# A graph block on one Trainium2 core: transpositions that write columns four apart, straight copies, and late work at other units

## The chip, the cores and the metric

The kernel runs on one core of a Trainium2 chip. TensorE (PE in the rows) multiplies matrices into PSUM, VectorE (DVE), ScalarE (ACT) and GpSimd (POOL) do elementwise work, SyncE (SP) issues transfers. Each engine runs its own list of instructions in order and waits on semaphores. The metric is the device time in microseconds (us), the median of several runs.

## The reference

```python
h = relu(layernorm(x))                       # x: 8192 x 128, fp32
deg = clip(adj.sum(axis=1), 1.0)             # adj: 8192 x 8192, zeros and ones
dis = deg ** -0.5
diffusion = (dis[:, None] * adj * dis[None, :]) @ h - h
norms = maximum(norm(h, axis=-1), 1e-8)
sim = h @ h.T / (norms[:, None] * norms[None, :])
attn = softmax(beta * sim * adj, axis=1)     # 8192 x 8192, over whole rows
out = x + diffusion + sigmoid(alpha) * (attn @ h - h)
```

## The kernel before, in words

The rows of x are cut into 64 tiles of 128. The first phase walks over 512 **units**: a panel of 1024 output rows (8 panels) against one tile of 128 rows. For unit n TensorE computes the 128 x 1024 cosines into one of two halves ("slots") of `cos_ps` (`cosines`, L814: six products with 512 columns, since each operand is split in two fp16 parts). VectorE multiplies them by the adjacency (`masked`, L696), ScalarE takes the exponential twice (L420 as fp16, L424 as fp32), GpSimd makes the fp16 rest of it (`rest`, L323), and TensorE adds 24 small products of these with h to `top_ps` (`sums`, L859 to L863). TensorE does `sums` of a unit three units after its `cosines` (LAG = 3). A second phase (L889) multiplies by the adjacency.

The cosines need **unit rows**, the rows of h divided by their norms, transposed. Eight tiles are one block. For a block VectorE or ScalarE writes the unit rows, TensorE transposes the eight tiles into a free slot of `cos_ps` (`transposed`, L790), and VectorE copies the slot to `uT_hi` (L609, a cast to fp16) and the remainder to `uT_lo` (L610). This is `copy_uT`. The copies also put the columns in an order in which every fourth column belongs together: they write every fourth fp16 value.

Only blocks 0 and 1 are made before the units begin; half of x is normalised by then. The rest is **late work**, put between the units by a table of unit numbers in each engine's loop: on VectorE the statistics of x and h (`stats_of_x`, `stats_of_h`, `mean_var`), the square sums (`late_square_sums`), the inverse roots by three Newton steps (`late_norms`, `late_shift`), the unit rows of a block (`late_unit_rows`, L597 and L598) and its copies; on ScalarE the normalising activations (`relu`, L365), first guesses of roots (L355) and the fp16 part of h (`head_of_h`, L375); on GpSimd `tail_of_h`. Such work sits behind the unit's own instructions and ahead of the next unit's. In steady state VectorE also turns a quarter of an adjacency chunk every fourth unit (L633) and sums rows in two of four (L640).

`AHEAD = {10: 2, 13: 3, 49: 4, ...}` says at which unit a block is transposed: at unit n TensorE waits until unit n-2 is masked, transposes the block into the slot that is free, computes the cosines of n into the other one once unit n-1 is masked, and may compute those of n+1 only when VectorE has copied the block out. TensorE can't be two units ahead of VectorE there. The scratch columns of PSUM that the late steps use are `late_ps`.

Of the kernel before, what the change touches and what calls it, by code (L numbers as in the profile page):

```python
# [5 lines left out]
P = 128  # L6
# [6 lines left out]
def gnn_block_kernel(nc, x, adj, alpha, beta, out):  # L13
# [8 lines left out]
    ALU = mybir.AluOpType  # L22
# [17 lines left out]
    READY = 2  # L40
    LAG = 3
# [7 lines left out]
    AHEAD = {10: 2, 13: 3, 49: 4, 52: 5, 65: 6, 68: 7}  # L49
# [21 lines left out]
    with ctx:  # L71
# [114 lines left out]
        u_ready = sem("u_ready")  # L186
        uT_done = sem("uT_done")
# [37 lines left out]
        def _(sp):  # L225
# [27 lines left out]
            for m in range(BLOCKS):  # L253
# [3 lines left out]
                if m in (12, 15):  # L257
                    keep_h(2 if m == 12 else 3)
# [30 lines left out]
        def _(pool):  # L289
# [40 lines left out]
            tails = {6: 4, 8: 5, 10: 6, 12: 7, 46: 8, 48: 9, 50: 10, 52: 11, 60: 12, 62: 13, 64: 14, 66: 15}  # L330
# [13 lines left out]
        def _(act):  # L344
# [32 lines left out]
            def unit_rows(hb):  # L377
                act.wait_ge(rnorm_ready, hb // 2 + 1)
                for s in range(8):
                    last = nc.scalar.activation(unit[hb][:, s, :], x_st[:, 8 * hb + s, :], ACT.Copy,  # L380
                                                scale=rnorm[:, 8 * hb + s:8 * hb + s + 1])
                last.then_inc(u_ready, 1)
# [12 lines left out]

            def copy_acc(run):
                panel, _, behind = RUNS[run]
                act.wait_ge(attn_done, 16 * behind)
                if run in (0, 4):

                    groups = 1 if run == 0 else CH
                    for g in range(groups):
                        act.wait_ge(h_kept[g], 16 * Q)
                    act.wait_ge(hlo_ready, 4 * groups)
                    act.wait_ge(u_ready, 2 * groups)
# [7 lines left out]
            for n in range(UNITS):  # L413
# [59 lines left out]
        def _(dve):  # L473
# [81 lines left out]
            def late_root(value, root, tmp, to):  # L555
                near = late_ps[:, 0:value.shape[-1]]
                link(nc.vector.tensor_copy(near, root))
                for step in range(3):
                    link(nc.vector.scalar_tensor_tensor(out=tmp, in0=value, scalar=-0.5, in1=near, op0=ALU.mult, op1=ALU.mult))
                    link(nc.vector.tensor_tensor(tmp, tmp, near, ALU.mult))  # L560
                    last = nc.vector.scalar_tensor_tensor(out=near if step < 2 else to, in0=tmp, scalar=1.5, in1=near,
                                                          op0=ALU.add, op1=ALU.mult)
                    if step < 2:
                        link(last)
                return last

            def late_shift():
                of = slice(32, TILES)
                dve.wait_ge(std_ready, 3)
                link(late_root(va[:, of], vb[:, of], vc[:, of], rstd[:, of]))  # L570
                link(nc.vector.tensor_copy(late_ps[:, 0:32], rstd[:, of]))
                nc.vector.scalar_tensor_tensor(out=shift[:, of], in0=mv[:, of, 0], scalar=-1.0, in1=late_ps[:, 0:32],
                                               op0=ALU.mult, op1=ALU.mult).then_inc(ln_ready, 1)
                dve.wait_ge(ln_ready, 3)

            def late_square_sums(g):
                of = slice(16 * g, 16 * (g + 1))
                link(mean_var_of_h(g))
                both = late_ps[:, 0:32].rearrange("p (s k) -> p s k", k=2)
# [6 lines left out]
            def late_norms(g):  # L586
                of = slice(16 * g, 16 * (g + 1))
                dve.wait_ge(norm_root, g + 1)
                late_root(ssq[:, of], vb[:, of], vc[:, of], rnorm[:, of]).then_inc(rnorm_ready, 1)
                dve.wait_ge(rnorm_ready, g + 1)  # L590

            def late_unit_rows(hb):
                of = slice(8 * hb, 8 * (hb + 1))
                dve.wait_ge(rnorm_ready, hb // 2 + 1)
                if hb > READY:
                    dve.wait_ge(uT_done, hb)
                link(nc.vector.tensor_copy(late_ps[:, 0:8], rnorm[:, of]))  # L597
# [331 lines left out]
```

## Time and profile before

| | |
|---|---|
| median of 3 runs | 1914.03 us (1913.74 to 1915.01) |
| profiled execution | 1914.11 us, span 1912.0 us |
| PE busy | 1834.0 us, 96% |
| DVE, ACT, POOL busy | 1269.6, 1278.5, 1271.4 us, 66 to 67% each |
| granted TensorE clock, mean | 0.992 |

Durations are of one profiled execution. The time of a run is the span and 2.1 us around it. A row's time runs from start to end of an instruction, and the ends overlap the next start a little: an instruction with a row of 1.22 us lets the next one start after 1.14 us. The masks (L696) count the units: the first is unit 0, and the n-th after it unit n.

### The profile page before, as it was taken

To read this page: it belongs to the slowest core of one execution; us is meant where nothing else is said; L and a number is where in the kernel's file an instruction comes from. 1 tells how busy PE (TensorE), PEld (TensorE's weight loads), DVE (VectorE), ACT (ScalarE), POOL (GpSimd) and SP (SyncE) were. 2 spreads that over 40 slices of the span, in tenths; PEclk is the share of its full clock that TensorE was granted. 3 is DMA by queue.
4 is the path that set the end of the run, shared out by engine and by line. 5 is a ranking of instruction groups with operands and counts; after the bars stand their busy time and mean duration, and the time that the engine had idled before them with its cause. 6 is when DMAs were issued, how large, how long until landed. Compare 5 with 4: busy or idle time off the path is not lost.

```text
span 1912.0 us, 44763 instructions
## 1 busy us (share of the span) xinstructions
PE 1834.0 (96%) x19534; PEld 1448.1 (76%) x19534; DVE 1269.6 (66%) x1590; ACT 1278.5 (67%) x1210; POOL 1271.4 (66%) x793
## 2 busy tenths in 40 slices
PE   1899889999999999999999999999999999999999
PEld 1576567777777777777777777777777888888888
DVE  6988997879878778777877877787777210111111
ACT  4689868888889888988988898899887000000000
POOL 4688779998999999999999999999883000000000
PEclk9999989999999999999999999999999999999999
DMA  9977657876798876788887767888536745554520
GB/s 155 154 100 97 99 76 99 105 105 89 100 114 101 107 100 90 100 98 105 103 105 102 100 89 101 99 106 101 116 89 232 248 173 180 170 200 166 208 101 12
DMA packets 190409, 229.39 MB, mean 120 GB/s; under 512 B 7940, under 2 KB 163588, under 8 KB 186116
## 3 DMA queue, kind: packets, MB, share of 16 engines
q0 software_dynamic: 135168, 67.13, 44.9%
q1 hardware_dynamic: 29380, 145.77, 20.7%
q10 hardware_dynamic: 25664, 13.63, 2.6%
q8 instruction: 153, 2.51, 0.5%
q14 instruction: 44, 0.36, 0.1%
HBM read 352.32 MB, written 75.50 MB: 224 GB/s over the span
## 4 chain that ended last, share of the span: by engine, by line
PE 88%; DVE 6%; ACT 3%; issue 1%; DMA 0%; SPq 0%; DVEq 0%; ACTq 0%
PE cos_ps L814 32%; PE cos_ps L889 12%; PE top_ps L889 12%; PE top_ps L859 11%; PE top_ps L863 11%; PE top_ps L861 11%; DVE xe L696 1%; ACT xe L424 1%; ACT ustage L420 1%; DVE uT_lo L610 1%; DVE uT_hi L609 1%; ACT asb L365 1%; DVE top_ps L640 1%; DMA asb<-x_in 0%; DVE ptmp L598 0%
## 5 line engine op out<-in xcount | busy, mean ns | idle before, releaser
L323 POOL TENSOR_TENSOR ustage<-xe,ustage 128x1024 f16<-128x1024 f32 x512 | 1096.7, 2145 | 163.3 <-ACT xe L424 156.4
L696 DVE TENSOR_TENSOR xe<-cos_ps,arena 128x1024 f32<-128x1024 f32 x512 | 626.6, 1224 | 253.6 <-PE cos_ps L814 160.9
L420 ACT ACTIVATE ustage<-xe,ebias,ab 128x1024 f16<-128x1024 f32 x512 | 635.6, 1241 | 173.2 <-DVE xe L696 169.1
L859 PE MATMUL top_ps<-h,ustage 128*128 128x129 f16 x4096 | 722.6, 221 | 7.8 <-POOL ustage L323 5.5
L863 PE MATMUL top_ps<-h,ustage 128*128 128x129 f16 x4096 | 722.1, 221 | 0.0
L861 PE MATMUL top_ps<-hlo,ustage 128*128 128x128 f16 x4096 | 721.7, 220 | 0.0
L424 ACT ACTIVATE xe<-xe,ebias,ab 128x1024 f32<-128x1024 f32 x512 | 628.6, 1228 | 0.0
L859 PEld LDWEIGHTS top_ps<-h,ustage 128*128 128x128 f16 x4096 | 402.1, 98 | 72.1 <-POOL ustage L323 17.2
L861 PEld LDWEIGHTS top_ps<-hlo,ustage 128*128 128x128 f16 x4096 | 402.1, 98 | 56.2 <-issue 0.8
L863 PEld LDWEIGHTS top_ps<-h,ustage 128*128 128x128 f16 x4096 | 402.1, 98 | 0.0
L814 PE MATMUL cos_ps<-uT_hi 128*128 128x512 f16 x1024 | 307.0, 382 | 23.7 <-DVE uT_lo L610 21.7
L640 DVE TENSOR_REDUCE top_ps<-arena 128x8 f32<-128x1024 uint16 x256 | 311.8, 1218 | 0.0
L814 PE MATMUL cos_ps<-uT_hi,uT_lo 128*128 128x512 f16 x1024 | 307.0, 382 | 0.0
L814 PE MATMUL cos_ps<-uT_lo,uT_hi 128*128 128x512 f16 x1024 | 306.5, 381 | 0.0
L814 PEld LDWEIGHTS cos_ps<-uT_lo,uT_hi 128*128 128x128 f16 x1024 | 116.4, 114 | 106.6 <-issue 2.7
L814 PEld LDWEIGHTS cos_ps<-uT_hi,uT_lo 128*128 128x128 f16 x1024 | 116.6, 114 | 106.2 <-issue 2.2
L302 POOL DMA_DIRECT2D arena<-adj_in_dram x256 | 171.2, 670 | 7.4 <-DMA asb<-x_in 7.4
L633 DVE STREAM_TRANSPOSE arena<-arena 128x1024 uint32<-128x1024 uint32 x128 | 158.0, 1234 | 0.0
L770 DVE SCALAR_TENSOR_TENSOR ptmp<-top_ps,dis,ptmp 128x128 f32<-128x128 f32 x64 | 19.5, 346 | 189.4 <-PE top_ps L889 188.8
L770 DVE SCALAR_TENSOR_TENSOR ptmp<-cos_ps,dis,ptmp 128x128 f32<-128x128 f32 x64 | 19.5, 347 | 158.6 <-PE cos_ps L889 158.0
L814 PEld LDWEIGHTS cos_ps<-uT_hi 128*128 128x128 f16 x1024 | 87.3, 113 | 27.3 <-DVE uT_lo L610 23.0
L889 PE MATMUL cos_ps<-uT_hi,arena 128*128 128x256 f16 x896 | 100.1, 275 | 2.8 <-DVE uT_hi L751 2.8
(110 smaller groups left out, 1044.8 us busy)
## 6 DMA issues: line engine op xcount, KB each, us to landing
arena<-adj_in_dram POOLq DMA_DIRECT2D x256, 256.0 KB, 8.4
at_scratch<-arena SPq DMA_DIRECT2D x128, 512.0 KB, 4.2
arena<-at_scratch SPq DMA_DIRECT2D x26, 2048.0 KB, 7.9
xe<-at_scratch SPq DMA_DIRECT2D x6, 2048.0 KB, 7.8
h_scratch<-asb SPq DMA_DIRECT2D x16, 256.0 KB, 11.2
arena<-h_scratch SPq DMA_DIRECT2D x16, 256.0 KB, 6.5
ustage<-h_scratch ACTq DMA_DIRECT2D x8, 512.0 KB, 5.3
ptmp<-x_in ACTq DMA_DIRECT2D x8, 512.0 KB, 6.8
```

The source lines that it names most:

```text
L302: pool.dma_start(rows8[k % RS][C * q:C * (q + 1), of, :], adj_v[panel][:, of, 2048 * ch + 512 * q:2048 * ch + 512 * (q + 1)]).then_inc(row ...
L323: nc.gpsimd.tensor_tensor(elo[:, n % ES, :], ef[:, n % XS, :], ehi[:, n % ES, :], ALU.subtract).then_inc(elo_done, 1)
L420: nc.scalar.activation(ehi[:, n % ES, :], xm[:, n % XS, :], ACT.Exp, bias=ebias[:, 0:1], scale=ab[:, 1:2]).then_inc(ehi_done, 1)
L424: nc.scalar.activation(ef[:, n % XS, :], xm[:, n % XS, :], ACT.Exp, bias=ebias[:, 0:1], scale=ab[:, 1:2]).then_inc(ef_done, 1)
L633: nc.vector.transpose(at_words[:, w, :].rearrange("p (a r) -> p a r", r=32), rows_words[k % RS][:, :, 32 * w:32 * (w + 1)]).then_inc(at_re ...
L640: nc.vector.tensor_reduce(out=pairs_ps[:, of], in_=rows_pairs[k % RS][:, 8 * part:8 * (part + 1), :], axis=AX.X, op=ALU.add).then_inc(rows ...
L696: nc.vector.tensor_tensor(xm[:, n % XS, :], cos_ps[:, slot_of(n), :], at8[:, m % W, :, n % B], ALU.mult).then_inc(x_done, 1)
L814: last = nc.tensor.matmul(cos_ps[:, slot_of(n), q * HALF:(q + 1) * HALF].rearrange("p (w z) -> p w z", w=W), own(mine, s), columns(src, pa ...
L859: nc.tensor.matmul(top_ps[:, bank, col:col + P + 1], head, h1[:, s, 0:P + 1], start=(first and t % 3 == 0), stop=final, skip_group_check=True)
L861: nc.tensor.matmul(top_ps[:, bank, col:col + P], head, hlo[:, s, :], start=False, stop=final, skip_group_check=True)
L863: last = nc.tensor.matmul(top_ps[:, bank, col:col + P + 1], tail, h1[:, s, 0:P + 1], start=False, stop=final, skip_group_check=True)
L889: return nc.tensor.matmul(acc2[panel % 2][:, t, :], slot8[k % SL][:, j // B, t * P:(t + 1) * P, j % B], y[s // 32][:, s % 32, :], start=(s ...
```

## The change

`copy_uT` writes straight, and the transpositions write every fourth column of the PSUM slot instead. The two first blocks of unit rows are made by two engines: block 0 by VectorE in one instruction, block 1 by ScalarE in eight, where ScalarE made both. Their order against other work of the start changes. The late work has other unit numbers: `AHEAD` is {18: 2, 22: 3, 56: 4, 60: 5, 73: 6, 77: 7}, `relu` comes one tile a unit over 32 units instead of two over 16, statistics of h too, the Newton steps one a unit. TensorE gets 40 fp32 products of the identity with itself (128 columns) into slot 0 of `cos_ps` before the first transposition, once the first 16 tiles are normalised.

```diff
+    WARM = 40
-    AHEAD = {10: 2, 13: 3, 49: 4, 52: 5, 65: 6, 68: 7}
+    AHEAD = {18: 2, 22: 3, 56: 4, 60: 5, 73: 6, 77: 7}
...
@@ ScalarE
             var_root(0)
-            relu(0, 0, 8)
-            relu(0, 8, 16)
+            relu(0, 0, 16)
             var_root(1)
-            relu(1, 0, 8)
             ssq_root(0)
-            unit_rows(0)
-            unit_rows(1)
+            second_unit_rows()
             head_of_h(0)
             head_of_h(1)
-            relu(1, 8, 16)
+            relu(1, 0, 16)
...
-                elif n == 33:
+                elif n == 24:
                     var_root(2, 2)
-                if 35 <= n < 43:
-                    relu(2, 2 * (n - 35), 2 * (n - 34))
-                elif 48 <= n < 56:
-                    relu(3, 2 * (n - 48), 2 * (n - 47))
+                if 29 <= n < 45:
+                    relu(2, n - 29, n - 28)
+                elif 45 <= n < 61:
+                    relu(3, n - 45, n - 44)
@@ VectorE
+            def first_unit_rows():
+                dve.wait_ge(rnorm_ready, 1)
+                nc.vector.tensor_tensor(unit[0], x_st[:, 0:8, :], rnorm[:, 0:8].unsqueeze(2).to_broadcast([P, 8, P]),
+                                        ALU.mult).then_inc(u_ready, 1)
...
             def copy_uT(hb, slot):
                 dve.wait_ge(uT_done, hb + 1)
-
                 of = slice(PW * hb, PW * (hb + 1))
-                src = cos_ps[:, slot, :].rearrange("d (w b y) -> d w b y", w=2, b=B)
-                hi = uT_hi[:, of].rearrange("d (w y b) -> d w b y", w=2, b=B)
-                lo = uT_lo[:, of].rearrange("d (w y b) -> d w b y", w=2, b=B)
-                link(nc.vector.tensor_copy(hi, src))
-                nc.vector.tensor_tensor(lo, src, hi, ALU.subtract).then_inc(uT_copied, 1)
+                link(nc.vector.tensor_copy(uT_hi[:, of], cos_ps[:, slot, :]))
+                nc.vector.tensor_tensor(uT_lo[:, of], cos_ps[:, slot, :], uT_hi[:, of], ALU.subtract).then_inc(uT_copied, 1)
...
-            stats_of_h(0, 0, 8)
-            early_shift(1)
-            stats_of_h(0, 8, 16)
+            for four in range(4):
+                stats_of_h(0, 4 * four, 4 * (four + 1))
             early_square_sums(0)
             early_norms(0)
-            stats_of_h(1, 0, 8)
+            first_unit_rows()
+            early_shift(1)
             copy_uT(0, 0)
             copy_uT(1, 1)
...
-                if 1 <= n < 5:
-                    stats_of_h(1, 2 * n + 6, 2 * n + 8)
-                elif 16 <= n < 32:
-                    g, o = 2 + (n - 16) // 8, (n - 16) % 8
+                if 1 <= n < 9:
+                    stats_of_h(1, 2 * n - 2, 2 * n)
+                elif 31 <= n < 47:
+                    stats_of_h(2, n - 31, n - 30)
+                elif 48 <= n < 64:
+                    stats_of_h(3, n - 48, n - 47)
+                if 6 <= n < 22:
+                    g, o = 2 + (n - 6) // 8, (n - 6) % 8
...
+                elif n in (12, 13, 14):
+                    late_norms(1, n - 12)
+                elif n in (50, 51, 52):
+                    late_norms(2, n - 50)
+                elif n in (67, 68, 69):
+                    late_norms(3, n - 67)
...
-                elif n in (8, 11, 47, 50, 63, 66):
-                    late_unit_rows({8: 2, 11: 3, 47: 4, 50: 5, 63: 6, 66: 7}[n])
+                elif n in (15, 19, 53, 57, 70, 74):
+                    late_unit_rows({15: 2, 19: 3, 53: 4, 57: 5, 70: 6, 74: 7}[n])
@@ TensorE
                 for t in range(8):
-                    last = nc.tensor.transpose(cos_ps[:, slot, t * P:(t + 1) * P], unit[hb][:, t, :], ident32[:, :])
+
+                    dst = cos_ps[:, slot, HALF * (t // B):HALF * (t // B + 1)].rearrange("d (y b) -> d b y", b=B)[:, t % B]
+                    last = nc.tensor.transpose(dst, unit[hb][:, t, :], ident32[:, :])
                 last.then_inc(uT_done, 1)
...
+            pe.wait_ge(relu_done, 16)
+            for k in range(WARM):
+                nc.tensor.matmul(cos_ps[:, 0, 0:P], ident32[:, :], ident32[:, :], start=True, stop=True)
             transposed(0, 0)
             transposed(1, 1)
```

VectorE around the first late block (block 2), before the change, from the mask of unit 8 to that of unit 10:

```order
L696 TENSOR_TENSOR xe<-cos_ps,arena 128x1024
L640 TENSOR_REDUCE top_ps<-arena 128x8
L597 COPY top_ps<-rnorm 128x8
L598 TENSOR_TENSOR ptmp<-asb,top_ps 128x1024
L696 TENSOR_TENSOR xe<-cos_ps,arena 128x1024
L633 STREAM_TRANSPOSE arena<-arena 128x1024
L609 CAST uT_hi<-cos_ps 128x2x4x128
L610 TENSOR_TENSOR uT_lo<-cos_ps,uT_hi 128x2x4x128
```

and of the change, from the unit rows in unit 15 to the mask of unit 18 (L693 is the mask, L606 and L607 the copies, L508 statistics of x):

```order
L598 COPY top_ps<-rnorm 128x8
L599 TENSOR_TENSOR ptmp<-asb,top_ps 128x1024
L693 TENSOR_TENSOR xe<-cos_ps,arena 128x1024
L637 TENSOR_REDUCE top_ps<-arena 128x8
L508 BN_STATS ptmp<-asb 128x6 x2
L693 TENSOR_TENSOR xe<-cos_ps,arena 128x1024
L630 STREAM_TRANSPOSE arena<-arena 128x1024
L508 BN_STATS ptmp<-asb 128x6 x2
L606 CAST uT_hi<-cos_ps 128x1024
L607 TENSOR_TENSOR uT_lo<-cos_ps,uT_hi 128x1024
L693 TENSOR_TENSOR xe<-cos_ps,arena 128x1024
```

Between unit rows and copies stand two masks now, where one stood; the copies' shape is flat; statistics of x stand in between.

ScalarE while the second half of x is normalised, before (units 35 to 37: two exponentials, then two tiles):

```order
L420 ACTIVATE ustage<-xe,ebias,ab 128x1024
L424 ACTIVATE xe<-xe,ebias,ab 128x1024
L365 ACTIVATE asb<-asb,shift,rstd 128x128 x2
L420 ACTIVATE ustage<-xe,ebias,ab 128x1024
L424 ACTIVATE xe<-xe,ebias,ab 128x1024
L365 ACTIVATE asb<-asb,shift,rstd 128x128 x2
```

and of the change (units 45 and 46, where a `head_of_h`, L377, stands too):

```order
L418 ACTIVATE ustage<-xe,ebias,ab 128x1024
L422 ACTIVATE xe<-xe,ebias,ab 128x1024
L377 ACTIVATE h<-asb 128x8x128
L367 ACTIVATE asb<-asb,shift,rstd 128x128
L418 ACTIVATE ustage<-xe,ebias,ab 128x1024
L422 ACTIVATE xe<-xe,ebias,ab 128x1024
L367 ACTIVATE asb<-asb,shift,rstd 128x128
```

Every unit has one tile now, and the run of such units is twice as long.

## Rows read from the trace of the kernel before

**Rows 1.** Windows: us from:to, length, busy (x instructions) by engine, PEclk, DMA, GB/s
```profile
47.41:121.02 73.61, 65.14 (x641) 46.42 (x640) 66.86 (x100) 55.62 (x51) 51.40 (x29) 0.93 0.80 121
121.02:298.35 177.33, 157.81 (x1684) 115.44 (x1682) 161.11 (x273) 145.65 (x154) 145.40 (x93) 0.97 0.73 100
298.35:1434.00 1135.65, 1134.76 (x12843) 863.55 (x12841) 907.93 (x792) 1020.65 (x872) 1038.56 (x629) 1.00 0.74 101
```

**Rows 2.** Waits of TensorE: who waited for whom, us in total, times, longest
```profile
PE cos_ps L814 <- DVE uT_lo L610: 21.7, 7, 7.7
```

**Rows 3.** Timeline of the start: start us, us, engine, line, names, count, idle before
```profile
15.93 6.26 ACT L365 ACTIVATE asb<-asb,shift,rstd 128x128 f32<-128x128 f32 x16 [2.12 <-DVE shift L527]
...
24.48 1.64 DVE L533 BATCH_NORM_STATS2 ptmp<-asb 128x6 f32<-128x128 f32 x8
...
26.14 1.17 DVE L538 BATCH_NORM_AGGREGATE hv<-ptmp 128x2 f32<-128x6 f32 x16
...
30.20 4.78 ACT L380 ACTIVATE xe<-asb,rnorm 128x128 f32<-128x128 f32 x16 [1.92 <-DVE rnorm L486]
...
32.79 1.94 PE L790 MATMUL cos_ps<-ident,xe 128*128 128x128 f32 x8 [28.44 <-ACT xe L380]
...
44.55 1.04 PE L814 MATMUL cos_ps<-uT_hi 128*128 128x512 f16 x2 [7.67 <-DVE uT_lo L610]
...
47.41 1.23 DVE L696 TENSOR_TENSOR xe<-cos_ps,arena 128x1024 f32<-128x1024 f32 x1 [1.86 <-PE cos_ps L814]
```

**Rows 4.** Timeline of VectorE, units 8 to 10
```profile
72.66 1.22 DVE L598 TENSOR_TENSOR ptmp<-asb,top_ps 128x1024 f32<-128x1024 f32 x1
73.92 1.22 DVE L696 TENSOR_TENSOR xe<-cos_ps,arena 128x1024 f32<-128x1024 f32 x1
75.06 1.23 DVE L633 STREAM_TRANSPOSE arena<-arena 128x1024 uint32<-128x1024 uint32 x1
76.22 2.44 DVE L609 CAST uT_hi<-cos_ps 128x1024 f16<-128x1024 f32 x1
...
80.93 1.24 DVE L696 TENSOR_TENSOR xe<-cos_ps,arena 128x1024 f32<-128x1024 f32 x1
```

**Rows 5.** Products with 128 fp32 rows of `degs` (four in the code), L831: ns min/median/max
```profile
L831 PE MATMUL top_ps<-degs,ptmp x8: 219/275/275, 1439.3 to 1440.1; 128*128 128x64 f32 x8
```

**Rows 6.** Window with TensorE's clock at half, around the first cosines
```profile
40.05:50.30 10.25, 5.75 (x14) 2.06 (x15) 8.16 (x6) 1.56 (x2) 0.31 (x1) 0.50 1.15 234
```

**Rows 7.** Timeline of TensorE: cosines of units 17 and 18; block 4 transposed
```profile
103.34 0.59 PE L814 MATMUL cos_ps<-uT_hi 128*128 128x512 f16 x2
103.78 0.59 PE L814 MATMUL cos_ps<-uT_lo,uT_hi 128*128 128x512 f16 x2
...
105.99 0.59 PE L814 MATMUL cos_ps<-uT_hi 128*128 128x512 f16 x2
...
194.90 1.07 PE L790 MATMUL cos_ps<-ident,ptmp 128*128 128x128 f32 x8 [2.33 <-DVE ptmp L598]
```

**Rows 8.** Timeline of VectorE: statistics of x; masks of units 23 and 78
```profile
104.52 0.48 DVE L510 BATCH_NORM_STATS2 ptmp<-asb 128x6 f32<-128x128 f32 x2
...
121.02 1.22 DVE L696 TENSOR_TENSOR xe<-cos_ps,arena 128x1024 f32<-128x1024 f32 x1 [0.76 <-PE cos_ps L814]
...
298.35 1.22 DVE L696 TENSOR_TENSOR xe<-cos_ps,arena 128x1024 f32<-128x1024 f32 x1 [0.27 <-DVE arena L633]
```

**Rows 9.** Timeline of ScalarE, units 35 and 36
```profile
158.82 0.86 ACT L365 ACTIVATE asb<-asb,shift,rstd 128x128 f32<-128x128 f32 x2
159.59 1.23 ACT L420 ACTIVATE ustage<-xe,ebias,ab 128x1024 f16<-128x1024 f32 x1
...
161.86 0.86 ACT L365 ACTIVATE asb<-asb,shift,rstd 128x128 f32<-128x128 f32 x2
```

**Rows 10.** The page's costliest groups: GpSimd's fp16 rest
```profile
L323 POOL TENSOR_TENSOR ustage<-xe,ustage 128x1024 f16<-128x1024 f32 x512 | 1096.7, 2145 | 163.3 <-ACT xe L424 156.4
```

**Rows 11.** One line: a cast of 512 columns to fp16, out of SBUF, L750
```profile
L750 DVE CAST uT_hi<-ptmp x8: 426/427/428, 1457.5 to 1465.7; 128x512 f16<-128x512 f32 x8
```

More of the change, by code:

```diff
@@ L186, in gnn_block_kernel @@
         u_ready = sem("u_ready")
+        u1_ready = sem("u1_ready")
         uT_done = sem("uT_done")
@@ L256, in _ @@
                 sp.dma_start(at_dram[m // W, :, 1024 * w:1024 * (w + 1)], at_words[:, w, :]).then_inc(at_stored[w], 16)
-                if m in (12, 15):
-                    keep_h(2 if m == 12 else 3)
+                if m in (13, 16):
+                    keep_h(2 if m == 13 else 3)
                 if m // W in (CHUNKS - 3, CHUNKS - 2) and w == W - 1:
@@ L327, in first_unit @@
                 return 16 * (k - RS) + (18 if k < 13 else 13)
-            tails = {6: 4, 8: 5, 10: 6, 12: 7, 46: 8, 48: 9, 50: 10, 52: 11, 60: 12, 62: 13, 64: 14, 66: 15}
+            tails = {7: 4, 9: 5, 11: 6, 13: 7, 48: 8, 50: 9, 52: 10, 54: 11, 64: 12, 66: 13, 68: 14, 70: 15}
             for n in range(UNITS):
@@ L375, in head_of_h, with second_unit_rows @@
                 nc.scalar.activation(h1[:, 8 * hb:8 * (hb + 1), 0:P], x_st[:, 8 * hb:8 * (hb + 1), :], ACT.Copy).then_inc(hhi_ready, 1)
[L377 to L382, printed above, removed]
+            def second_unit_rows():
+                act.wait_ge(rnorm_ready, 1)
+                for s in range(8, 16):
+                    last = nc.scalar.activation(unit[1][:, s - 8, :], x_st[:, s, :], ACT.Copy, scale=rnorm[:, s:s + 1])
+                last.then_inc(u1_ready, 1)
             var_root(0)
-            relu(0, 0, 8)
-            relu(0, 8, 16)
+            relu(0, 0, 16)
             var_root(1)
-            relu(1, 0, 8)
             ssq_root(0)
-            unit_rows(0)
-            unit_rows(1)
+            second_unit_rows()
             head_of_h(0)
             head_of_h(1)
-            relu(1, 8, 16)
+            relu(1, 0, 16)
             def copy_acc(run):
@@ L552, in early_norms, with late_step @@
                 refine_root(ssq[:, of], vb[:, of], vc[:, of], rnorm[:, of]).then_inc(rnorm_ready, 1)
-            def late_root(value, root, tmp, to):
+            def late_step(value, root, tmp, to, step):
                 near = late_ps[:, 0:value.shape[-1]]
[L557 to L565, printed above, removed]
@@ L567, in late_shift @@
-            def late_shift():
-                of = slice(32, TILES)
[L569 to L574, printed above, removed]
+                if step == 0:
+                    link(nc.vector.tensor_copy(near, root))
@@ new lines, in late_step, with late_scale @@
+                link(nc.vector.scalar_tensor_tensor(out=tmp, in0=value, scalar=-0.5, in1=near, op0=ALU.mult, op1=ALU.mult))
+                link(nc.vector.tensor_tensor(tmp, tmp, near, ALU.mult))
+                link(nc.vector.scalar_tensor_tensor(out=near if step < 2 else to, in0=tmp, scalar=1.5, in1=near,
+                                                    op0=ALU.add, op1=ALU.mult))
+            def late_scale(step):
+                of = slice(32, TILES)
+                if step == 0:
+                    dve.wait_ge(std_ready, 3)
+                if step < 3:
+                    late_step(va[:, of], vb[:, of], vc[:, of], rstd[:, of], step)
+                else:
+                    link(nc.vector.tensor_copy(late_ps[:, 0:32], rstd[:, of]))
+                    nc.vector.scalar_tensor_tensor(out=shift[:, of], in0=mv[:, of, 0], scalar=-1.0, in1=late_ps[:, 0:32],
+                                                   op0=ALU.mult, op1=ALU.mult).then_inc(ln_ready, 1)
+                    dve.wait_ge(ln_ready, 3)
@@ L576, in late_square_sums @@
             def late_square_sums(g):
                 of = slice(16 * g, 16 * (g + 1))
-                link(mean_var_of_h(g))
-                both = late_ps[:, 0:32].rearrange("p (s k) -> p s k", k=2)
+                both = late_ps[:, 32:64].rearrange("p (s k) -> p s k", k=2)
                 link(nc.vector.tensor_copy(both, hv[:, of, :]))
```

48 lines of the change are left out of this document (23 added, 25 removed).

## The prediction

> **What bounds the kernel now.** I read the windows first, then TensorE's waits, then the timelines. From unit 78 on (298.35 us) TensorE is busy 1134.76 of 1135.65 us [rows 1]: it is the bound, and nothing of the change lies there. Cosines of one unit start 2.65 us after those of the last, with 2 x 0.215 us a pair, 1.29 us in all [rows 7]; so 1.36 us are `sums`. The change can win only ahead of unit 78: 47.4 us until the first mask, 73.6 us until the mask of unit 23, 177.3 us until that of unit 78 [rows 1, 3, 8]. In the latter two TensorE would need 59 (below) and 55 x 2.65 + 4 x 1.07 = 150 us with six blocks transposed. What it loses there shows in its waits: 21.7 us for the copies of blocks [rows 2], 2.33 us at a time for unit rows [rows 7], and in the granted clock of 0.93 and 0.97 [rows 1]. For the start, the timeline shows one chain: normalise, statistics of h, root, unit rows, transposition, four copies, cosines [rows 3].
>
> **How late an engine may be.** From the end of `cosines(n)` to the start of `cosines(n+2)` there are 2 x 2.65 - 1.29 = 4.0 us; the mask of n takes 1.2 of them, so VectorE may be 2.8 us late without TensorE's noticing. From the end of `cosines(n)` to `sums(n)` there are 3 x 2.65 = 7.95 us; mask, two exponentials (2.27 us [rows 9] and an end of 0.1) and GpSimd's 2.15 us [rows 10] take 5.8, so ScalarE may be 2.1 us late. At a unit in AHEAD the first allowance shrinks: from the mask of n-1 to the copies' end VectorE needs 1.14 for the mask, 1.15 for a sum of rows (the turn's time [rows 4]) and the copies.
>
> **The copies.** Each takes 2.44 us, two cost 4.71 us from 76.22 to the mask at 80.93 [rows 4]. The mask reads as many fp32 columns of the same PSUM tile and writes straight, in 1.22 us, and lets go after 1.14 [rows 4]. I take 1.2 us a copy, 2.4 a block. Below, the cast could be as quick as the one from SBUF, 2 x 0.43 us for 1024 columns [rows 11], a gain of 0.3 us more a block; above, it stays at 2.44 if PSUM and not the stride is the reason. The Trainium skill (Advanced Engine Details and Errata, Memory Cachelines) gives SBUF lines of 16 bytes and full speed with two hits on one; a step of four fp16 values would then be free and the copies not get faster. The twofold time of the strided copies beside the mask speaks against that reading.
>
> **The transpositions.** Eight take 1.07 us at full clock [rows 7] and 1.94 at half [rows 3]. No row shows TensorE writing every fourth column. I take no cost: 0.114 us a pass for 128 columns is more than twice what a pass of the cosines takes a column, so the write has room. Below I exclude a gain. Above, VectorE's factor of two for a stride: 1.07 us a block, 8.6 us for eight.
>
> **The start.** Statistics of the last tiles of h stand at 24.48 us for 1.64 us [rows 3], behind the second root chain. Now they follow as tiles are normalised, the last at 15.93 + 6.26 = 22.2 us; twelve of sixteen are through at 22.9, the last four at 23.8. The aggregation starts 2.35 us earlier, so do the norms: 27.85 for 30.20. Block 0 takes VectorE 1.22 us (as L598 [rows 4]; the root chain that follows it, 2.1 us, is over at 31.2), block 1 takes ScalarE 8 x 0.3. Both are ready by 30.3 instead of 35.0.
> TensorE isn't: the 40 products start at 22.3. A product of fp32 is two passes: four products of L831 are eight rows [rows 5]. A pass costs 0.114 us at full clock and 0.213 at half, by the transpositions; a product 0.23 or 0.43. In this trace TensorE went on at 1.2 GHz for 5.75 us of work from 44.55 before 2.4 GHz was granted at 50.30 [rows 3, 6]. The same here: 13 products at half and 27 at full, 5.75 + 6.2, end at 34.2. Between all at full (31.4, later than the unit rows still) and all at half (39.5) lies this cost. Transpositions end at 35.3 and 36.4, four copies at 35.3 + 4.8 = 40.1, against 44.55. Then the cosines: TensorE has idled 3.7 us by then. It fell to half after the idle 7.7 us before 44.55 [rows 3], and kept full after a wait of 2.33 at 194.90 [rows 7]; between them I take the middle. The first mask came 2.86 us behind the first cosines; at full clock 1.6. So it stands at 41.7 to 43.0; I take 42.5. Gain 4.9 us.
>
> **Units 0 to 22.** VectorE is the bound here. Steady work a unit: 907.93 us over 428 units is 2.12 of rows, less 0.08 for each of 1.85 instructions: 1.97 us [rows 1]; 23 units, 45.4 us. Late work: 24 pairs of statistics at 0.51 (0.48 and the link [rows 8]), 12.3; one aggregation with square sums and root, 4.1 (26.14 to 30.20 [rows 3]; ScalarE's guess falls out, scratch copies come in), two aggregations more at 1.18, 2.4; two blocks of unit rows at 1.44, 2.9; two blocks of copies, 4.8. Sum 71.9 us. TensorE's own need is 3.9 + 20 x 2.65 + 2.1 = 59. VectorE ends 12.9 us behind, of which TensorE doesn't feel 2.8. So unit 23 stands at 42.5 + 69.1 = 111.6 for TensorE instead of 121.02: 4.4 us more, though nine pairs of statistics of x more than before are done by then.
>
> **Units 23 to 77.** ScalarE: two tiles cost 0.77 us on top of 2.27, 3.04 a unit [rows 9], over TensorE's 2.65, eight times in each of two stretches. One tile is 0.39 (6.26 us for 16 [rows 3]): 2.66, no loss. On top come, from unit 45 on, two `head_of_h` (1.9), a root (0.2), the copies of the accumulator (1.1) and 0.6 of excess; 3.8, less 2.1 of allowance, 1.7 us lost. The Newton steps of unit 50 may find that root late: 1.4.
> VectorE, block 4 to 7: unit rows now come three units ahead, so TensorE's 2.3 us wait [rows 7] goes. At a block from the mask of n-1: 1.14 + 1.15 + 2.4 = 4.7 us against the 4.0 + 1.07 that TensorE spends anyway; only lateness counts. Adding late work unit by unit against 2.65 I get it 1.6, 1.5, 1.8 and 0.2 us late at units 55, 59, 72 and 76, each less 0.4: 3.7 us lost in all; and 1.0 at units 53 and 65 over the allowance. Before, the same sum was 1.14 + 1.15 + 4.71: 1.9 us plus the lateness, with the wait for unit rows ahead.
> Loss 1.7 + 1.4 + 3.7 + 1.0 = 7.8, so 150 + 7.8 = 158 us instead of 177.3: 19.5 us. No stall is over 2 us, so I count on full clock; the 0.97 of before [rows 1] is in its 177.3.
>
> **Sum.** 4.9 + 4.4 + 19.5 = 28.8 us off the profiled execution's 1914.1 (span 1912.0 and 2.1), which stands at the median, 1914.03. Predicted 1885 us. GpSimd's tails, SyncE's `keep_h` and row loads keep their relation to units; adjacency rows of unit 16 are there well ahead.
>
> **Rivals.**
> *The late work gives back half* (chance 0.20): waits between ScalarE and VectorE add up where both run full, units 29 to 60, and stalls still drop the clock. For it: 0.39 us a unit leave ScalarE no slack for 32 units. Against: allowances of 2 to 3 us. Half of 19.5 stays: 1895 us.
> *The copies stay at 2.4 us* (0.06): 2.3 us a block, at all eight: 18 us, 1903. Against: the mask's 1.22.
> *Strided writes cost by VectorE's factor two* (0.08): up to 8.6 us, 1889 to 1894.
> *Slower than before* (0.03): each transposed column written four apart is much slower. It decides from 28.8 / 8 = 3.6 us a block more, 4.7 instead of 1.07, that is 0.59 us a pass; at eight times the pass, 8.6 us a block, all behind a wait, 1885 + 60 = 1945. For it: nothing in the trace. The Trainium skill (same page and section) says that PSUM has 8-byte lines and that a pattern that isn't contiguous slows matmuls markedly; by that rule this case has its chance, and no row here shows such a write.
> *The products gain nothing* (in the range, not apart): without them cosines would start at 36 at half clock; they cost about what they give, 2 to 4 us.
> Forecast as worked out: 0.63.
>
> **Numbers.** The forecast's own range is 1878 to 1891: below, losses of 1 us instead of 7.8; above, first cosines 2 us later and 4 us more stalls. With the rivals the range of 8 in 10 is 1877 to 1899. Faster by over 0.2% (3.8 us, about what a measurement of this kernel tells from no change): 0.95; within: 0.02; slower: 0.03.
>
> **What would show it.** Copies at 1.2 us a row; transpositions at 1.07 us a block; the first product at 22.3 and the last at 34; first cosines near 40, first mask at 41.7 to 43; the mask of unit 23 near 114, that of 78 near 270; waits for L607 under 8 us, none for unit rows in the units; PEclk near 1 from unit 5 on. It is wrong if copies stay over 2 us, if a transposed block takes over 2 us, if VectorE's busy share between the first mask and that of 23 is under 9 in 10, or if the time after unit 78 changes.

## The result and the profile after

| | before | changed |
|---|---|---|
| median | 1913.95 us (4 runs) | 1891.82 us (4 runs, 1890.3 to 1892.5) |
| ratio | | 0.9882, 95% interval 0.9865 to 0.9899 |
| profiled execution, span | 1914.1, 1912.0 us | 1890.3, 1888.2 us |
| first mask | 47.41 us | 41.65 us |
| mask of unit 23 | 121.02 | 115.80 |
| mask of unit 78 | 298.35 | 276.78 |

The change is 22.1 us faster; 28.8 us were forecast. The time lies inside the range of 8 in 10 (1877 to 1899) and 0.8 us above the forecast's own range (1878 to 1891). The windows of the changed kernel, cut at its masks of units 0, 23 and 78, and then a stretch as long as the third of [rows 1] (us from:to, length, busy by engine, PEclk, DMA, GB/s), against [rows 1]:

```profile
41.65:115.80 74.15, 63.99 (x637) 44.55 (x636) 70.38 (x159) 55.66 (x52) 53.75 (x30) 0.96 0.97 151
115.80:276.78 160.98, 153.87 (x1697) 114.98 (x1695) 146.95 (x223) 144.77 (x153) 143.46 (x91) 0.99 0.78 104
276.78:1412.43 1135.65, 1134.75 (x12842) 863.53 (x12840) 908.09 (x793) 1020.89 (x873) 1038.89 (x628) 1.00 0.75 101
```

The long stretch is the same to a hundredth of a us. Units 0 to 22 take 74.15 us, 0.5 more than before; the next 55 take 161.0 for 177.3. With 5.8 us at the start that is 21.6 us, and 22.1 at unit 81, where the masks are in step again. TensorE's waits between 40 and 280 us are to be read against [rows 2]. Two more lines of the kernel before (40 to 300 us) come first, then the changed kernel's:

```profile
PE cos_ps L790 <- DVE ptmp L598: 6.9, 3, 2.3
PE top_ps L859 <- POOL ustage L323: 3.7, 12, 0.6
```
```profile
PE cos_ps L822 <- DVE xe L693: 5.7, 6, 1.7
PE top_ps L867 <- POOL ustage L325: 5.4, 10, 1.0
PE cos_ps L822 <- DVE uT_lo L607: 3.3, 3, 2.4
PE top_ps L867 <- ACT asb L406: 2.5, 1, 2.5
PE cos_ps L798 <- DVE xe L693: 0.3, 1, 0.3
```

Of the 21.7 us for the copies 7.7 stood at the first cosines and 14.0 in the units; here it is 4.1 (at 38.88 us, before this window) and 3.3. The wait for unit rows, 6.9 us before, is gone, and GpSimd is near the top, with 5.4 us for 3.7. The copies themselves, by line (ns min/median/max), against [rows 4]; then a transposed block of the changed kernel at full clock, against [rows 7]:

```profile
L606 DVE CAST uT_hi<-cos_ps x8: 1215/1224/1225, 33.9 to 272.1; 128x1024 f16<-128x1024 f32 x8
L607 DVE TENSOR_TENSOR uT_lo<-cos_ps,uT_hi x8: 1224/1224/1225, 35.2 to 273.4; 128x1024 f16<-128x1024 f32 x8
```
```profile
106.01 1.05 PE L798 MATMUL cos_ps<-ident,ptmp 128*128 128x128 f32 x8
```

The start in the timeline, against [rows 3]:

```profile
16.09 6.26 ACT L367 ACTIVATE asb<-asb,shift,rstd 128x128 f32<-128x128 f32 x16 [2.13 <-DVE shift L525]
...
20.48 3.59 DVE L531 BATCH_NORM_STATS2 ptmp<-asb 128x6 f32<-128x128 f32 x16
...
22.49 10.54 PE L878 MATMUL cos_ps<-ident 128*128 128x128 f32 x80 [17.75 <-ACT asb L367]
...
28.15 1.22 DVE L591 TENSOR_TENSOR xe<-asb,rnorm 128x1024 f32<-128x1024 f32 x1
...
32.87 1.91 PE L798 MATMUL cos_ps<-ident,xe 128*128 128x128 f32 x16
33.94 1.23 DVE L606 CAST uT_hi<-cos_ps 128x1024 f16<-128x1024 f32 x1 [2.60 <-PE cos_ps L798]
...
38.88 0.96 PE L822 MATMUL cos_ps<-uT_hi 128*128 128x512 f16 x2 [4.10 <-DVE uT_lo L607]
...
41.65 1.23 DVE L693 TENSOR_TENSOR xe<-cos_ps,arena 128x1024 f32<-128x1024 f32 x1 [1.68 <-PE cos_ps L822]
```

L878 are the idle products. Block 0's unit rows are there at 29.4 us, and the products hold TensorE until 32.9. Behind the transpositions TensorE idles 4.1 us, and the clock falls for the first cosines. The half clock (a granted share of 0.50, 1.2 of 2.4 GHz) stands in three stretches up to unit 23, each behind a stall; the windows are cut inside them:

```profile
39.10:42.40 3.30, 3.30 (x9) 1.22 (x8) 1.62 (x2) 0.00 (x0) 0.00 (x0) 0.50 1.13 232
93.70:97.00 3.30, 3.30 (x14) 1.63 (x15) 3.23 (x5) 2.25 (x2) 2.65 (x2) 0.50 0.40 156
114.20:117.50 3.30, 3.30 (x23) 2.46 (x22) 2.07 (x3) 2.81 (x3) 0.45 (x1) 0.50 1.19 94
```

The later two are the blocks at units 18 and 22: TensorE's timeline there shows waits of 1.69 and 2.40 us.

```profile
93.61 1.04 PE L822 MATMUL cos_ps<-uT_hi 128*128 128x512 f16 x2 [1.69 <-DVE xe L693]
...
113.49 0.63 PE L822 MATMUL cos_ps<-uT_hi 128*128 128x512 f16 x2 [2.40 <-DVE uT_lo L607]
```

The same two waits don't always have a half clock behind them. e3 below has the same instructions up to unit 23, the same waits of 1.69 us (to 94.76) and 2.40 us (to 114.38), and full clock behind both:

```profile
94.80:98.20 3.40, 2.79 (x30) 1.99 (x30) 3.33 (x5) 2.88 (x4) 2.76 (x2) 1.00 0.39 151
114.40:117.80 3.40, 3.40 (x34) 2.46 (x35) 2.90 (x3) 2.31 (x3) 0.00 (x0) 1.00 1.19 96
```

### The profile page after: what moved, and what is told of

Same layout as the page of the kernel before. It is cut to its first block, busy times and chain, and to the rows that moved or that the text cites. A ratio compares the mean times of both kernels' runs of the same rounds, so it can differ in the third digit from the quotient of the medians.

```text
span 1888.2 us, 44938 instructions
## 1 busy us (share of the span) xinstructions
PE 1835.1 (97%) x19614; PEld 1453.3 (77%) x19614; DVE 1253.8 (66%) x1591; ACT 1274.9 (68%) x1202; POOL 1272.0 (67%) x793
## 4 chain that ended last, share of the span: by engine, by line
PE 87%; DVE 4%; ACT 3%; POOL 3%; issue 2%; DMA 0%; SPq 0%; DVEq 0%; POOLq 0%
PE cos_ps L822 31%; PE cos_ps L901 12%; PE top_ps L901 12%; PE top_ps L867 11%; PE top_ps L871 11%; PE top_ps L869 10%; POOL ustage L325 2%; ACT xe L422 1%; ACT ustage L418 1%; DVE xe L693 1%; DVE top_ps L637 1%; ACT asb L367 1%; PE cos_ps L878 1%; DVE ptmp L508 0%; POOL arena L304 0%
## 5 line engine op out<-in xcount | busy, mean ns | idle before, releaser
L693 DVE TENSOR_TENSOR xe<-cos_ps,arena 128x1024 f32<-128x1024 f32 x512 | 626.5, 1224 | 248.2 <-PE cos_ps L822 159.7
L867 PEld LDWEIGHTS top_ps<-h,ustage 128*128 128x128 f16 x4096 | 401.4, 98 | 73.2 <-POOL ustage L325 17.0
L773 DVE SCALAR_TENSOR_TENSOR ptmp<-top_ps,dis,ptmp 128x128 f32<-128x128 f32 x64 | 19.5, 347 | 189.4 <-PE top_ps L901 188.8
L773 DVE SCALAR_TENSOR_TENSOR ptmp<-cos_ps,dis,ptmp 128x128 f32<-128x128 f32 x64 | 19.5, 347 | 157.8 <-PE cos_ps L901 157.2
```

The source lines that it names most:

```text
L693: nc.vector.tensor_tensor(xm[:, n % XS, :], cos_ps[:, slot_of(n), :], at8[:, m % W, :, n % B], ALU.mult).then_inc(x_done, 1)
L867: nc.tensor.matmul(top_ps[:, bank, col:col + P + 1], head, h1[:, s, 0:P + 1], start=(first and t % 3 == 0), stop=final, skip_group_check=True)
```

## The experiments

Each ran on a chip with the kernel before; times are medians. "From the first mask" cuts the start off. The changed kernel itself ran again as the mark: 1891.28 us, against 1914.09 of before.

> The changed kernel once more, as the mark for its variants on the same chip. Expected as measured: 1891.8 us, 22 us under the kernel before; first mask at 41.65, unit 81's mask at 284.16 us. Both theories expect the same.

Measured: 1891.28 us as expected, but its profile differs from the first one's in where the half clock falls: it shows two more stretches of it, at 192.5 and 1438.3 us; the mask of unit 81 stands at 285.2 instead of 284.2, and the whole execution is 2.75 us longer. So 1 us in one profile is no evidence on the whole time; what is read below is the time from the first mask and the medians. From the first mask to that of unit 24 the two profiles agree better, 77.7 us each.

**Copies and transpositions, each way.**

```diff
-                    dst = cos_ps[:, slot, HALF * (t // B):HALF * (t // B + 1)].rearrange("d (y b) -> d b y", b=B)[:, t % B]
-                    last = nc.tensor.transpose(dst, unit[hb][:, t, :], ident32[:, :])
+                    last = nc.tensor.transpose(cos_ps[:, slot, t * P:(t + 1) * P], unit[hb][:, t, :], ident32[:, :])
...
-                link(nc.vector.tensor_copy(uT_hi[:, of], cos_ps[:, slot, :]))
-                nc.vector.tensor_tensor(uT_lo[:, of], cos_ps[:, slot, :], uT_hi[:, of], ALU.subtract).then_inc(uT_copied, 1)
+                src = cos_ps[:, slot, :].rearrange("d (w b y) -> d w b y", w=2, b=B)
+                ...
```

> The changed kernel with the transpositions and copies of before: VectorE writes every fourth value again, TensorE writes straight. Theory A (TensorE's strided write is free, VectorE's strided write costs 2.3 us a block): a block of transpositions takes the same 0.114 us a pass, copies 2.44 us; start 4.7 us later, each of six late blocks 2.3 to 2.9 us with the half clock that its longer wait brings: 18 to 22 us slower than the changed kernel, 1911. Theory B (the other parts hide half of the copies): 10 us slower, 1902.

> The kernel before with the transpositions and copies of the change alone. Theory A (the copies are most of the gain): 4.9 us at the start and 2.3 to 2.8 us at each of six blocks, 18 to 22 us faster than before, 1894, so the other parts together are worth 2 us. Theory B (the schedule and the copies share it): 12 us faster, 1902.

Measured: the changed kernel with the old copies takes 1915.65 us, 1.0013 of before (1.0004 to 1.0022); the kernel before with the new copies 1892.38, 0.9886 (0.9872 to 0.9899). So the copies alone give 21.9 us. The rest of the change costs 1.4 us without them, and with them it gives 0.6 to 1.1 us, which is inside the spread. Theory B falls both times; the old copies cost the changed kernel 24.4 us, more than theory A's 18 to 22.

The rest isn't idle, though: it moves time about. From start to first mask, to the mask of unit 23, to that of unit 78, the copies alone save 5.1, 6.8 and 10.2 us against the kernel before; the whole change saves 5.8, -0.5 and 16.3. At unit 81 both stand within 0.1 us of each other (284.19 and 284.16). The other parts lose in units 0 to 22 what they win later. In the first of the two, the copies' line and the transpositions':

```profile
L609 DVE CAST uT_hi<-cos_ps x8: 2433/2466/2484, 34.6 to 293.3; 128x1024 f16<-128x1024 f32 x8
```
```profile
L800 PE MATMUL cos_ps<-ident,ptmp x48: 272/273/332, 96.3 to 292.9; 128*128 128x128 f32 x48
```

The cast takes twice the time with its strided output; TensorE's row has the same median, 273 ns, as when it writes four apart (272 to 327, median 273, in the changed kernel). So the stride of four costs a factor of two in VectorE's fp16 output and nothing in what these fp32 transpositions write. A straight write with the old copies' four-dimensional pattern was not tried; the unit rows' instruction, whose pattern is 8 x 128 with a broadcast operand, takes 1.22 us [rows 4] (out of SBUF, straight, to fp32), so more dimensions alone need not cost. The Trainium skill (Advanced Engine Details and Errata, Memory Cachelines) says that any non-contiguous pattern in PSUM slows matmuls significantly, and that two hits on an SBUF line of 16 bytes keep full speed, which would make four fp16 values a free stride; the measurements differ from both, and they decide. Matmuls with a cheaper pass were not tried.

**The idle products.**

```diff
-    WARM = 40
+    WARM = 0        # e2: 16
```

> The 40 idle products are left out. Theory A (they cost about what they give or more): the first transposition is no longer held until 32.9 us; it starts at about 29.5 at half clock, the copies end at 36.2 instead of 38.8, the first mask stands at 39 instead of 41.65; VectorE is the bound in the units that follow, so TensorE's half clock there costs nothing: 2.0 to 2.6 us faster than the changed kernel, 1889.4. Theory B (the products pay by the clock): without them TensorE stays at 1.2 GHz for 5.75 us of work behind the first cosines, first mask at 41.5 or later, and 1 to 3 us slower than the changed kernel.

> 16 idle products instead of 40: they end near 27.8 us, ahead of the unit rows at 29.4. Theory A (an idle product is worth nothing once its end is ahead of the unit rows, but the transpositions run at full clock): transpositions 29.5 to 31.6, first cosines at 36.2, first mask at 38.5 to 39.4, as without products or up to 0.8 us sooner, 1887.5. Theory B (what makes products pay is that TensorE does not stop before the transpositions): the clock falls and the first mask stands at 39.4 as without products or later, 1888.

Measured: 1887.87 us without, 1887.91 with 16; 3.4 us under the changed kernel. The timeline without them:

```profile
29.59 3.43 PE L798 MATMUL cos_ps<-ident,xe 128*128 128x128 f32 x16 [24.61 <-DVE xe L591]
...
36.50 1.04 PE L822 MATMUL cos_ps<-uT_hi 128*128 128x512 f16 x2 [3.48 <-DVE uT_lo L607]
...
39.36 1.23 DVE L693 TENSOR_TENSOR xe<-cos_ps,arena 128x1024 f32<-128x1024 f32 x1 [1.76 <-PE cos_ps L822]
```

Transpositions at half clock, and the first mask 2.3 us sooner all the same. The products' clock doesn't last to the first cosines: from there to the first mask it is 2.77 us with 40 products and 2.86 without. With 16 products the transpositions take 2.33 us for 3.43, the cosines start at 35.69 and the first mask stands at 38.54, as theory A said; the half clock there lasts from 34.7 to 41.5 and the median is the same. Since VectorE sets the units that follow (next experiments), TensorE's clock buys nothing at this place that the medians show. Of the 3.4 us, 2.3 are the start and about 0.2 up to unit 24. The profiles don't show where the rest is; this execution is 2.5 us shorter than the changed kernel's, and the medians differ more.

**Units 0 to 23: whose time is it?**

```diff
-                    stats_of_x(g, 2 * o, 2 * (o + 1))      # e10
+                    if o == 0:
+                        stats_of_x(g, 0, 1)
...
-                    if o == 7:                             # e6
+                    if n == 13:
                         link(mean_var(g))
+                if n == 22:
+                    link(mean_var(3))
```

> The changed kernel with 30 of the 32 statistics of x in units 6 to 21 left out (the normalisation of half of x is computed from wrong sums). Theory A (VectorE's sum of work sets units 0 to 22): 15 x 0.51 = 7.6 us less work, mask of unit 24 6 to 7.6 us sooner behind the first, 1885. Theory B (the two blocks' waits set them, whatever stands between): 1 to 2 us sooner, 1890.

> The last aggregation of x (1.17 us on VectorE) moved from unit 21, ahead of the copies of block 3, to unit 22, behind its mask. Theory A (at a block every us of VectorE ahead of the copies is TensorE's wait, and the wait of 2.4 us brings the half clock at 114.1): the wait falls to 1.2, the half clock there goes, the mask of unit 24 comes 1.2 to 2.9 us sooner, 1889.5. Theory B (the stretch is VectorE's sum of work, whatever its order): the mask of unit 24 stands where it stood, 1891.8.

Measured: without the statistics the mask of unit 24 comes 70.0 us behind the first instead of 77.7: 7.7 us for 7.6 us of work left out. Median 1882.16; the work left out is work the kernel needs, so this is a test and no gain. VectorE's sum of work is the bound. Its window from first mask to that of unit 24 (the changed kernel has 73.82 of 77.73 us busy, and PEclk 0.95):

```profile
41.40:111.41 70.01, 65.49 (x690) 47.12 (x689) 67.46 (x131) 58.63 (x54) 55.74 (x31) 0.98 1.05 162
```

With the aggregation moved, that mask comes 76.2 us behind the first, 1.5 sooner; the wait at the block is 1.20 us for 2.40. Six profiles with the aggregation at its old place and the same work (the changed kernel twice, e1, e2, e3, e7) have 77.3 to 77.7, and e9 below, which moves it too, has 76.0. So order at a block counts, by 1.1 to 1.5 us. No half clock shows there, but that isn't the aggregation's doing: e2, e3 and e7 keep the 2.40 us wait and show none behind it either. The median is 1891.77, above the 1889.5 of theory A: in this profile the first mask stood at 43.03, with a half clock of 6.8 us at the start, and another fell at 191.9. The total can't tell these two theories apart, the stretch does.

**GpSimd, later.** e3 has the tails of groups 2 and 3 at other units.

```diff
-            tails = {..., 48: 8, 50: 9, 52: 10, 54: 11, 64: 12, 66: 13, 68: 14, 70: 15}
+            tails = {..., 46: 8, 47: 9, 48: 10, 49: 11, 62: 12, 63: 13, 64: 14, 65: 15}
```

> GpSimd's tails of h at units 46 to 49 and 62 to 65 instead of 48 to 54 and 64 to 70, ahead of its row loads at 50 to 57 and 66 to 73. Theory A (GpSimd became the bound in units 50 to 77, since a load of 0.67 us and every second unit a tail of 1.1 us stand on 2.14 us): TensorE's waits for GpSimd's rest fall from 5.4 to under 2 us, the mask of unit 81 comes 2.5 to 4 us sooner, 1888.5. Theory B (VectorE's late work bounds these units anyway, GpSimd is only next in line): under 1 us sooner, 1891.

Measured: 1888.92 us, 2.4 under the mark; from the mask of unit 24 to that of 81, 162.3 us for 164.8 (164.1 to 166.2 in the profiles of the changed kernel, e1, e2 and e6). TensorE's wait for GpSimd falls from 5.4 to 3.2 us, less than I expected, and its wait for copies in the units grows from 3.3 to 5.9; of 2.5 us these rows show little, so that part of the account stays open. GpSimd's timeline in the changed kernel, units 51 to 54:

```profile
201.48 0.67 POOL L304 DMA_DIRECT2D arena<-adj_in_dram  x1
202.16 2.16 POOL L325 TENSOR_TENSOR ustage<-xe,ustage 128x1024 f16<-128x1024 f32 x1
204.27 1.13 POOL L316 TENSOR_TENSOR hlo<-asb,h 128x512 f16<-128x512 f32 x1
205.34 0.67 POOL L304 DMA_DIRECT2D arena<-adj_in_dram  x1
206.02 2.15 POOL L325 TENSOR_TENSOR ustage<-xe,ustage 128x1024 f16<-128x1024 f32 x1
208.11 0.67 POOL L304 DMA_DIRECT2D arena<-adj_in_dram  x1
```

No idle time: the rest, a row load's issue and a tail are 3.9 us in a unit of 2.65. With the tails moved there is idle time again within the loads:

```profile
205.80 0.67 POOL L304 DMA_DIRECT2D arena<-adj_in_dram  x1
207.10 2.14 POOL L325 TENSOR_TENSOR ustage<-xe,ustage 128x1024 f16<-128x1024 f32 x1 [0.63 <-ACT xe L422]
```

The tables explain it. GpSimd issues row loads in units 50 to 57 and 66 to 73, in both kernels. Before, three of the eight tails of groups 2 and 3 stood in such units (50, 52, 66); the change moved the tails, and six do (50, 52, 54, 66, 68, 70); in e3 none does. GpSimd from its rest of unit 50 to that of unit 58 (fifth of the busy times) in the kernel before, the changed one and e3:

```profile
209.57:235.94 26.37, 23.85 (x258) 16.93 (x256) 23.99 (x31) 23.89 (x30) 24.24 (x18) 1.00 0.88 105
```
```profile
195.55:220.96 25.41, 24.09 (x259) 17.61 (x258) 24.44 (x34) 22.18 (x26) 25.32 (x20) 1.00 0.94 110
```
```profile
195.39:220.15 24.76, 23.54 (x258) 17.85 (x257) 23.83 (x32) 21.52 (x25) 22.07 (x16) 1.00 1.02 117
```

It had 2.1 us to spare before, has 0.1 in the changed kernel and 2.7 in e3.

**ScalarE, and the old units.** e7 normalises two tiles a unit (units 29 to 36 and 45 to 52); e8 puts all late work back at the units of before.

```diff
-                if 29 <= n < 45:
-                    relu(2, n - 29, n - 28)
+                if 29 <= n < 37:                            # e7
+                    relu(2, 2 * (n - 29), 2 * (n - 28))
...
-    AHEAD = {18: 2, 22: 3, 56: 4, 60: 5, 73: 6, 77: 7}      # e8, and all other unit numbers
+    AHEAD = {10: 2, 13: 3, 49: 4, 52: 5, 65: 6, 68: 7}
```

> The changed kernel with two tiles normalised a unit on ScalarE, in units 29 to 36 and 45 to 52, instead of one in 29 to 60. Theory A (one tile a unit fits in TensorE's 2.65 us, two don't): ScalarE takes 3.04 us a unit, 3.1 us in each stretch over TensorE's time, of which an allowance of 2.1 is not felt in the first; the second meets the accumulator's copies: 3 to 5 us slower than the changed kernel, 1895.5. Theory B (VectorE and GpSimd set these units): within 1 us, 1892.

> The changed kernel (start, copies, 40 products) with the late work at the units of the kernel before; only the statistics of h of the second group, which the start no longer begins, come four a unit in units 1 to 4. Theory A (the new units are worth about nothing: they cost 4 us up to unit 24, where statistics of x now stand ahead of blocks 2 and 3, and give 4 to 6 back later): 1892 to 1895, the mask of unit 24 74 to 76 us behind the first instead of 77.7, that of unit 81 245 instead of 242.5. Theory B (the new units save what I counted, 8 us and more, and the products and the start ate it): 1900 or more.

Measured: e7 1896.36 us, 5.1 over the mark, at the upper end of theory A: ScalarE goes at 3.04 us a unit again, and the accumulator's copies make TensorE wait 3.9 us instead of 2.5.

```profile
152.47 0.87 ACT L367 ACTIVATE asb<-asb,shift,rstd 128x128 f32<-128x128 f32 x2
153.24 1.23 ACT L418 ACTIVATE ustage<-xe,ebias,ab 128x1024 f16<-128x1024 f32 x1
...
155.51 0.87 ACT L367 ACTIVATE asb<-asb,shift,rstd 128x128 f32<-128x128 f32 x2
```

e8 takes 1893.41 us: with quick copies the old units cost 2.1 us in all. Its first mask stands at 41.75 and that of unit 24 here:

```profile
114.56 1.23 DVE L693 TENSOR_TENSOR xe<-cos_ps,arena 128x1024 f32<-128x1024 f32 x1
```

That is 72.8 us behind the first for 77.7, below theory A's 74 to 76; the mask of unit 81 comes 244.6 us behind for 242.5, as theory A said. So the old units are 4.9 us better up to unit 24 and 7.0 us worse from there to 81 (171.8 for 164.8). By unit 24 they have done eight pairs of statistics of x less (0.51 us each) and one aggregation less (1.18 us), 5.3 us of VectorE's work. The table of new units, which looked like the bulk of the change, is a trade: it spares ScalarE and the wait for unit rows later (in e8 TensorE waits 7.0 us for them), and pays with work of VectorE put ahead of two blocks. It nets 2 us.

**Together.** e9: no products, the aggregation at 22, tails at 39 to 48 and 58 to 64, heads of h at 38, 45, 54, 61. e11: no products, blocks 2 and 3 ahead of most statistics of x, everything later over more units (other lines change with it):

```diff
+    AHEAD = {13: 2, 17: 3, 63: 4, 67: 5, 79: 6, 83: 7}
+    tails = {7: 4, 9: 5, 11: 6, 13: 7, 47: 8, 49: 9, 58: 10, 60: 11, 63: 12, 65: 13, 74: 14, 76: 15}
...
+                if 14 <= n < 30:
+                    g, o = 2 + (n - 14) // 8, (n - 14) % 8
...
+                if 37 <= n < 53:
+                    relu(2, n - 37, n - 36)
+                elif 53 <= n < 69:
+                    relu(3, n - 53, n - 52)
```

> The changed kernel without products, with the last aggregation of x at unit 22, GpSimd's tails of groups 2 and 3 at 39 to 48 and 58 to 64, and ScalarE's heads of h at 38, 45, 54 and 61. If the single gains add (3.4 for the products, 2.5 for the tails, 1.5 for the aggregation, and up to 1 of the wait of 2.5 us for the accumulator's copies): 1884. If VectorE's sum of work takes them back: 1887, as without products alone.

> Without products; blocks 2 and 3 at units 13 and 17, ahead of most statistics of x (now units 14 to 29), normalising at 37 to 68, blocks 4 to 7 at 63, 67, 79 and 83, tails of h at units without row loads. Theory A (VectorE's work up to unit 24 is too much and later units have room): the mask of unit 24 comes 73 to 74 us behind the first, that of unit 87 4 to 6 us sooner than in the changed kernel besides the products' 3 us: 1883. Theory B (the sum up to the last block is the bound however it is spread, 1.97 us a unit and the late work): 1887.

Measured: e9 1885.17 us, 6.1 under the mark; of the 8.4 us that the single gains sum to, 6.1 arrive, between the two theories (1884 and 1887). e11 1881.97 us, 0.9833 of before (0.9818 to 0.9847), 9.3 under the changed kernel's mark and the fastest of the kernels that do all the work. Unit 24's mask stands 70.3 us behind the first, about 3 us better than theory A said, since work was moved behind it; from there to unit 87 it takes 180.5 us, as in the changed kernel (180.7). The mask of unit 87 stands at 289.7 us instead of 300.1, so the later units did have room. TensorE's waits from 34 to 300 us:

```profile
PE cos_ps L825 <- DVE uT_lo L607: 5.1, 3, 3.3
PE cos_ps L825 <- DVE xe L693: 4.1, 5, 1.5
PE top_ps L870 <- POOL ustage L325: 2.3, 5, 0.9
PE top_ps L870 <- ACT asb L406: 1.8, 2, 1.3
PE cos_ps L801 <- DVE ptmp L599: 1.7, 1, 1.7
...
```

## Why the prediction was right, and where it was not

- **As a whole**: the direction, the copies' time and the size of the gain were right, within 6.7 us. The shares weren't: 4.9, 4.4 and 19.5 us forecast for the start, units 0 to 22 and the rest; 5.8, -0.5 and 16.3 measured, and 0.6 more up to unit 81. That the total comes near what the copies give alone (22.1 and 21.9) is not something the prediction worked out; its other parts cancel.
- **Copies**: right, 1.22 us each, and so was the free strided write. That this term alone is the whole result was not seen; what the copies give by themselves was never set apart from the rest of each stage.
- **Start**: 4.9 us forecast, 5.8 measured. The products ended at 32.9 instead of 34.2: the half clock ended at 25.4, 2.9 us behind their start, where I had taken 5.75. Five other profiles with the same start have 3.1 to 5.9 us there and the first mask at 41.25 to 43.39, so the forecast's 42.5 lies in the spread. The first cosines ran at half clock after an idle 4.1 us. I called the products neutral; they cost 3.4 us. The step that failed is "they cost about what they give". They give 0.1 us: without them the first cosines start 2.4 us sooner and the first mask follows them 2.86 us later instead of 2.77, and TensorE's time in the units behind is not what bounds them.
- **Units 0 to 22**: VectorE's sum of 71.9 us is 71.9: 74.15 measured, with 2.2 us in which it waited (0.15, 0.84 and 1.23). What failed is "of which TensorE doesn't feel 2.8". A block stands at unit 22, and at a block that allowance is gone, as the same text says for later ones. The waits are the rest of the 5 us, and only part of them is the clock: e3, at full clock in the same units from 44.7 us on, takes 73.2 us and VectorE waits 1.1.
- **The clock**: "no stall is over 2 us, so I count on full clock", said of the later units, failed in its premise: waits of 2.40 and 2.48 us stand in the changed kernel. The reasoning from a wait's length doesn't hold either. Waits of 1.69 and 2.40 us had a half clock behind them here and none in e3. The trace of before already had both: the prediction took the 2.33 us wait at 194.90 that kept full clock [rows 7], and the same wait at the first late block had the half clock from 74.2 to 77.6 us behind it:

```profile
74.03 1.81 PE L790 MATMUL cos_ps<-ident,ptmp 128*128 128x128 f32 x8 [2.33 <-DVE ptmp L598]
```

- **Units 23 to 81**: 166 us forecast with stalls of 7.8, 168.4 measured, so 10.1 over TensorE's own need as I had worked it out. The rows of waits show 7.2 of them: GpSimd 3.5 (the other 1.9 of its 5.4 stand in units 0 to 22), the accumulator's copies 2.5 where I had 1.7, copies 0.9 where I had 3.7, since VectorE was less late than counted, and a mask 0.3. The remaining 2.9 us no row shows; the half clock until 117.5 is part of them. GpSimd I had put aside with "GpSimd's tails [...] keep their relation to units". That step failed: the change moves the tails and not the row loads, so six tails instead of three fall together with a load.
- The sum of these, -0.9 + 5.0 + 2.4, is the 6.6 us between the forecast 277.6 for the mask of unit 81 and the measured 284.2. The rival that half of the late work's gain is lost was the nearest (1895), but for its cause: not ScalarE but the order at the first blocks and GpSimd.
- In the profiled executions the difference is 23.8 us, not 22.1: before the change a half clock of 3.4 us stood at 1460 us, between the phases, and none here. The changed kernel's second profile has one at that place too (1438.3 us).

## What to carry to other kernels

Price each part of a change by itself: a stride in one engine's write gave as much here as the whole change, and the rest netted 0.6 to 1.1 us: the products cost 3.4, the new units gave 2.1, and what is left over, some 2 us by subtraction, would be the start's new order. A clock is worth having only where its engine is the bound in the units that follow. When a stall is taken away, add up every engine's work in the unit that is now shorter, those too that seemed to have room, and check which of its tasks now meet in one unit; and spend an allowance between engines once, not again at a place that has a barrier.

## What the hardware showed beside this

- A small instruction of VectorE with operands in SBUF alone (`va`, 32 columns) took 0.17 us in the kernel before (in unit 32) and 0.55 to 1.90 us in the ten profiles that have it in unit 23. In all ten it begins inside an instruction of GpSimd's and ends within 0.05 us of that one's end; before, it began as GpSimd's ended. In the changed kernel:

```profile
118.07 1.17 DVE L732 TENSOR_SCALAR va<-mv 128x32 f32<-128x32 f32 x1
```
```profile
117.05 2.14 POOL L325 TENSOR_TENSOR ustage<-xe,ustage 128x1024 f16<-128x1024 f32 x1 [3.63 <-ACT xe L422]
```

  The Trainium skill (SBUF — State Buffer, Who interferes with whom) says that VectorE and GpSimd share one pair of SBUF ports as an exclusive lock, that a tensor_scalar of VectorE can be one of the instructions that take it, and that the later one is then blocked for the whole instruction of the other. 117.05 + 2.14 = 119.19 and 118.07 + 1.17 = 119.24 agree with it. By these rows it costs 1.0 us at unit 23, because of where that instruction now stands; in e11, where it begins ahead of GpSimd's in unit 31, it takes 0.17 again. It was not tried alone.
- The same program shows the half clock at other places in each run. In six kernels whose start is identical (the changed kernel twice, e3, e6, e7, e10) the first mask stands at 41.25 to 43.39 us, and the changed kernel's two profiles, with one half clock more at 192.5 us and one at 1438.3, are 2.75 us apart.
